# Third probability tile of each softmax row-sum buffer added by an accumulating DMA instead of a GpSimd tensor addition

## The reference, cut to what matters

```python
# layer 0
energy = einsum('bhqd,bhkd->bhqk', q, k)
att = softmax(energy, axis=-1) / D ** 0.5
out = einsum('bhqk,bhkd->bhqd', att, v)
# layer 1
attn = softmax(einsum('bhqd,bhkd->bhqk', q, k) * hd ** (-0.5), axis=-1)
o = einsum('bhqk,bhkd->bhqd', attn, v)
```

## Time and profile before

| | us |
|---|---|
| median of 3 runs | 2860.76 |
| lowest and highest run | 2857.95, 2862.33 |
| span of the profiled execution | 2861.9 |
| PE busy | 2668.9 (93%) |
| POOL busy | 2007.3 (70%) |
| DVE busy | 2205.5 (77%) |
| ACT busy | 1843.9 (64%) |

### The profile page before, as it was taken

The page is one execution under the profiler, slowest core; times in us unless marked ns, Lnnn a source line. Parts: engine busy times, 40 slices in busy tenths (PEclk is TensorE's granted clock), DMA queues, the critical chain, the costliest instruction groups (busy, mean ns, idle before and its releaser), DMA issues. The chain is left out here.

```text
span 2861.9 us, 62235 instructions
## 1 busy us (share of the span) xinstructions
PE 2668.9 (93%) x22273; PEld 1492.6 (52%) x22273; DVE 2205.5 (77%) x4467; ACT 1843.9 (64%) x3329; POOL 2007.3 (70%) x1695
## 2 busy tenths in 40 slices
PE   7899999998999989999759998999899899959998
PEld 5655466554665547555325554554455455524444
DVE  5778678776888768878577868776877787749998
ACT  4366555665556655566456677667766776657997
POOL 0399724996269951799439997998799799965442
PEclk9999999999999999999879999999999999989999
DMA  6122443223432425323222314322332222252000
GB/s 229 38 58 63 149 122 101 57 69 133 142 92 57 123 76 161 75 58 90 74 78 60 77 32 115 80 57 58 88 79 63 66 75 57 50 207 95 33 29 37
DMA packets 102198, 243.55 MB, mean 85 GB/s; under 512 B 18828, under 2 KB 25108, under 8 KB 101016
## 3 DMA queue, kind: packets, MB, share of 16 engines
q1 hardware_dynamic: 100120, 233.49, 28.8%
q0 software_dynamic: 1792, 6.33, 0.6%
HBM read 99.15 MB, written 38.88 MB: 48 GB/s over the span
## 5 line engine op out<-in xcount | busy, mean ns | idle before, releaser
L502 DVE TENSOR_REDUCE a_mxs<-ps 128x1 f32<-128x512 f32 x2048 | 1268.5, 682 | 258.2 <-PE ps L371 255.8
L463 ACT ACTIVATE a_p<-ps 128x512 f32<-128x512 f32 x2048 | 1042.4, 607 | 203.8 <-PE ps L385 194.2
L340 POOL TENSOR_TENSOR a_sum<-a_p 128x512 f32<-128x512 f32 x768 | 987.9, 1293 | 87.0 <-PE ps L403 73.5
L371 PE MATMUL ps<-a_k,a_q 96*128 96x512 f32 x2048 | 855.6, 424 | 27.9 <-DVE a_mxs L502 24.4
L385 PE MATMUL ps<-a_q,a_k 98*128 98x512 f32 x2048 | 810.2, 419 | 19.1 <-ACT a_p L463 11.6
L345 POOL TENSOR_TENSOR a_sum<-a_sum,a_p 128x512 f32<-128x512 f32 x512 | 663.8, 1296 | 40.2
L403 PE MATMUL ps<-a_sum,a_unit 128*32 128x512 f32 x1536 | 656.9, 599 | 16.4 <-POOL a_sum L345 13.1
L403 PE MATMUL ps<-a_p,a_vx 128*32 128x512 f32 x4096 | 664.1, 599 | 1.7 <-DVE tok L521 1.6
L371 PEld LDWEIGHTS ps<-a_k,a_q 96*128 96x128 f32 x2048 | 389.1, 190 | 262.9 <-DVE a_mxs L502 109.6
L385 PEld LDWEIGHTS ps<-a_q,a_k 98*128 98x128 f32 x2048 | 384.2, 189 | 257.6 <-ACT a_p L463 162.0
L472 ACT ACTIVATE a_ots<-ps 128x512 f32<-128x512 f32 x256 | 152.6, 597 | 419.4 <-PE ps L403 418.7
(11 more groups left out here) (249 smaller groups left out, 3149.9 us busy)
## 6 DMA issues: line engine op xcount, KB each, us to landing
a_q<-qh SPq DMA_DIRECT2D x256, 128.0 KB, 2.3
a_k<-kh SPq DMA_DIRECT2D x256, 128.0 KB, 2.4
a_q<-ql SPq DMA_DIRECT2D x128, 128.0 KB, 2.3
a_k<-kl SPq DMA_DIRECT2D x128, 128.0 KB, 2.4
x<-a_p SPq DMA_DIRECT2D x64, 256.0 KB, 2.1
a_p<-in_w_fc SPq DMA_DIRECT2D x12, 1024.0 KB, 8.5
kh<-in_x SPq DMA_DIRECT2D x4, 2048.0 KB, 14.6
a_p<-x SPq DMA_DIRECT2D x16, 512.0 KB, 6.0
```

Source lines behind the costliest of these rows:

```text
L340: pair = pool.tensor_tensor(tile, self.key_tile(u, kt), self.key_tile(u, kt + 1), ALU.add)
L371: pe.matmul(self.mx[self.mx_ring[at]], self.q[j][0:96, t * P:(t + 1) * P], self.k[j][0:96, half * HALF:(half + 1) * HALF], start=True, sto ...
L463: act.activation(self.key_tile(u, kt), self.st[self.st_ring[CHUNKS * k + n]], ACT.Exp, scale=self.scale).then_inc(self.s_exp, 1)
L502: dve.reduce_max(self.mxs[:, k % 2, c:c + 1], self.mx[self.mx_ring[CHUNKS * k + c]], axis=AX.X).then_inc(self.s_mxr, 1)
```

## The change

The third tile is no longer added by a GpSimd instruction. GpSimd begins a DMA that reads the probability tile (128 partitions by 512 fp32, 256 KB) and adds it into the buffer in SBUF. Its completion is counted on a semaphore of its own for each half and buffer, and PE waits for that in the rounds that read such a buffer. The wait for `s_part` stays, now ahead of the DMA. The two-tile buffers are as before. Round 8 reads two buffers (j = 8 and 9) and now has two waits where it had one.

```diff
+        self.s_third = [[sem(f"third{u}{r}") for r in range(2)] for u in range(2)]
...
             pair.then_inc(self.s_part, 1)
             pool.wait_ge(self.s_part, 2 * (2 * N + u) + r + 1)
             pool.wait_ge(self.s_exp, CHUNKS * N + TT * u + kt + 2 + 1 + self.EXP_CREDIT)
-            pool.tensor_tensor(tile, tile, self.key_tile(u, kt + 2), ALU.add).then_inc(self.s_sum, 1)
+            pool.dma_start(tile, self.key_tile(u, kt + 2), accum_op=ALU.add).then_inc(self.s_third[u][r], 16)
...
-        pe.wait_ge(self.s_sum, 2 * self.PER_HALF * E + used[-1] + 1)
+        for j in used:
+            head, u, part = E + j // (2 * self.PER_HALF), j // self.PER_HALF % 2, j % self.PER_HALF
+            if part < 2:
+                pe.wait_ge(self.s_third[u][part], 16 * (head + 1))
+            else:
+                pe.wait_ge(self.s_sum, 2 * head + u + 1)
```

## The result

The changed kernel takes 3191.34 us (median of 4 runs, 3188.91 to 3193.41) against 2861.55 (4 runs, 2857.95 to 2863.47) for the kernel before on the same chip. The ratio is 1.1146, 95% interval 1.1132 to 1.116: 11.5% slower. The forecast was 2898 us with a range of 2850 to 3000. The direction was right, and so was the tightest place; the size was wrong by a factor of nine: +330 us in place of +37.

A forecast was written before the change was run, and what follows sets the result against it. PE was taken to bound the kernel, full in steady attention. The sum was 2861.9 + 42 us of waits at round 4 (48 x 0.87) - 5 us saved at batch ends = 2899, 2898 against the runs' median; range 2850 to 3000.

The forecast's parts named there:

- the ceiling of 15.7 us: PE's waits for POOL before L403, at batch ends: all a lighter GpSimd can give, 0.5%; 5 us credited.
- c: Time POOL spends on one DMA issue in place of a third addition: 0.7 us, bounds 0.56 to 1.1.
- the 0.8 us that was named as a sign of being wrong: Forecast is wrong if additions behind a DMA issue on POOL start later than 0.8 us after it.
- POOL gains nothing: Rival: an issue holds POOL 1.1 us; about 1.5 us for each of 64 pairs, 96 us, 2957 us; chance 0.16.
- L: Issue to landing of the accumulating DMA: 2.9 us alone, 4.1 in the burst of SP's six loads, bound 5.3 there.
- the prediction's other case: One packet for each 2 KB row, 8 for each engine: turns with SP's loads add 2.4 us, landing 5.3 us.
- the prediction's formula: PE's wait at round 4 for buffer j = 4: c + L + 2.85 - 6.78 us, forecast 0.87 us in 48 pairs.
- Round 9, "no wait": Buffer j = 10, read in round 9: DMA out at 1634.9, 4.25 us less 0.15 left, no wait at 4.1 us landing.
- The 16 pairs without head loads, priced at nothing: Two of each batch's eight pairs: landing of 2.9 us gives -0.33 us at round 4, so no wait.
- Accumulating is slow in itself: Rival: twice the DMA work, landing 6.6 us in the burst, 4.2 alone; 177 us of waits, 3040 or more; chance 0.10.
- Hidden after all: Rival: DMA lands within 3.2 us even in the burst, no new wait, 2846 to 2856 us; chance 0.18.
- no change: Rival: landing in the burst 3.3 to 3.5 us, 48 waits up to 0.2 us, 2855 to 2867 us; chance 0.14.

The follow-up runs named there:

- no_third: The kernel before with its 512 third additions left out and no DMA in their place: 2846.1 us, ratio 0.9925.
- plain_copy: The changed kernel with the DMA copying the third tile over the buffer instead of adding it: 2932.2 us, ratio 1.0225.
- late_sum: As no_third, without any DMA, but GpSimd adds the third tile of buffer 4 five times over: 3082.5 us, ratio 1.0761.

## Why the prediction was wrong, by its own steps

**What bounds the kernel: right.** PE sets the pace; the ceiling of 15.7 us is what no_third found, within about 5 us.

**The cost on POOL: the issue right, its neighbours missed.** c was taken as 0.7 in 0.56 to 1.1. The issue is recorded as 0.87 us, and the next addition starts 0.59 us after its start, inside the bounds and under the 0.8 us that was named as a sign of being wrong. But each issue begins 0.30 us after the addition ahead of it, where the next addition used to begin after 0.07, and the addition behind it takes 1.6 us in place of 1.28. The chain from buffer 3's first addition to j = 4's DMA was reckoned as 1.35 + 0.7 + 1.35 = 3.40 us; it is 1.57 + 0.59 + 1.91 = 4.07, where the third addition used to start after 3.96. Taken with its neighbours an issue therefore frees GpSimd nothing here, which is the half of "POOL gains nothing" that came true. Its busy time fell from 2007.3 to 1816.5 us, not to about 1700.

**L: mis-sized, and the step that failed most.** Alone it is 3.2 to 3.3 us rather than 2.9, inside the bounds. In the burst it is 5.7 in the mean rather than 4.1, above the upper bound of 5.3. The assumed packets of 4 KB fit this difference: the queue's 75520 packets, less the 1792 of before, are 144 for each DMA. The page counts 8192 more packets under 512 B than before (27020 against 18828), 16 for each DMA, so 128 are left, 2 KB each for 256 KB. That is 8 for each engine, the prediction's other case, which adds 2.4 us for the turns: 3.3 + 2.4 = 5.7. plain_copy has 80 packets a DMA by the same reckoning, so 64 of 4 KB and 4 for each engine, which would add 1.2 us; there buffer 4's landing is 3.7 us in the mean against 2.2 at best. Both agree with the taking of turns that the prediction assumed. No run shows the turns themselves.

**The deadline: right.** Round 4 was the tightest and round 9 the next. With the measured terms the prediction's formula gives 4.07 + 5.7 + 0.15 - 6.78 = 3.1 us. The recorded idle time starts only at the end of the matmul ahead and is 0.2 us shorter than such a delay; its mean in the first six pairs is 136.9 / 48 = 2.85. Forecast was 0.87. A wait is a difference: the two errors, 0.7 us in the chain and 1.6 in L, were each a part of its own term and as large as the wait or larger. Its price would have been 48 x 2.85 = 137 us in place of 42.

**Round 9, "no wait": wrong.** It waited 56.2 us. By the rows, 1639.30 - 1634.9 = 4.40 us, less 0.15, were left for the landing; the prediction's 4.25 is that figure with the 0.15 already off. Against L = 4.1 the margin was 0.15 us. In the first six pairs the DMA went out 3.8 us (median) before PE stood ready, since the issues ahead of it freed nothing, and landed after 4.6 us in the mean. Waits at rounds other than 4 were a sign of being wrong by the prediction's own words.

**The 16 pairs without head loads, priced at nothing: wrong, and a step that was not seen at all.** They waited 57 us, because the absence of head loads was taken for idle DMA engines; the DMAs of buffers 3 and 4 took up to 12.2 and 13.7 us there. The page of before listed SP's 2 MB transfer `kh<-in_x`, 14.6 us to landing.

**The clock, not considered: the largest omission.** 103 of 330 us. That PE has no idle time in which to catch up was said; that a wait also slows what follows it was not. late_sum shows it without any DMA.

**Rivals.** "Accumulating is slow in itself", chance 0.10, gave 3040 or more and came nearest, with L 4.2 alone and 6.6 in the burst against 3.3 and 5.7. It had the right consequence (several buffers wait, 177 us of waits at least) from too high a price. "POOL gains nothing" summed 1.5 us over all 64 pairs, though by its own terms the 16 without loads wait 0.07 us; 48 pairs give 72 us in place of 96. "Hidden after all" and "no change" fell with the landing above 3.5 us in the burst. The Trainium skill ("DMA: Bandwidth & Descriptors", section "Anatomy of one DMA - SWDGE (gpsimd) path") has the formula that was set beside the first of them, 2.0 us plus the bytes over 436 GB/s, so 2.6 us for 256 KB as an estimate; a plain copy landed in 2.2 us at best and 2.5 in the median, the accumulation in 3.2 at best, so the measurement goes against it for the accumulating kind.

**Sum of the account.** Round 4 of 48 pairs 137 us, round 9 of the same 44, other rounds there 4, the two late pairs 57, clock 103, less the 15.7 that POOL no longer costs: 329, against 328.6 us between the spans.

## What to carry to other kernels

When PE is full, an operation moved from a compute engine to a DMA can buy only the waits that PE has for that engine, and adds a latency that is paid at the tightest buffers; reckon the slack of every buffer, and price at the upper bound any whose slack is within 1 us of the latency. In these runs waits of PE that were mostly 2 to 3 us long cost 0.4 to 0.5 of their length again in half-clock work (71 us on 167.5 in late_sum, 103 on 226 in the changed kernel); behind waits under 1 us the clock fell once in 35 in the changed kernel. Before calling a stretch quiet, list every transfer in it by size, not only those of the loop at hand; and if a buffer is too tight, look first at which tile it is put in.

## What the runs showed of the hardware

- An accumulating DMA begun by GpSimd from SBUF to SBUF: issue 0.87 us whatever its size (32 or 256 KB), a plain copy 0.55.
- The addition behind an accumulating issue takes 1.6 us in place of 1.28; behind a plain copy's issue 1.29.
- A DMA of GpSimd that needs an addition's result is issued 0.30 us after it, where an addition follows after 0.07.
- Landing at best: 3.2 us accumulating 256 KB, 2.2 for a copy of it, 2.1 accumulating 32 KB. Beside a burst of six 128 KB loads 5.7 in the mean of 48, beside 2 MB loads 7.8 in one case, at most 13.7.
- 256 KB accumulated took the 16 engines (25.4% x 3190.5 - 0.6% x 2861.9) / 512 = 1.55 us; the copy by the same reckoning (12.9% of 2928.8) 0.70.
- Behind one wait of PE for 2.46 us the matmuls of the same round ran at half rate; of 58 waits of 2 us or more 42 went with a fall of the granted clock, of 74 shorter ones nine; over the whole run the time at the lower level grew by 206 us.
